# Attention and expert layer on one core: in the late attention steps VectorE computes three exponential tiles, ScalarE sixty in groups of three and one alone

## The reference, cut to what matters

```python
xn = layernorm(x)                                  # x: (4, 1024, 128)
q, k, v = heads(xn @ Wq.T), heads(xn @ Wk.T), heads(xn @ Wv.T)   # 16 heads of 8
q, k = rope(q), rope(k)
attn = softmax(einsum('bhnd,bhmd->bhnm', q, k) * 8 ** -0.5)
a = einsum('bhnm,bhmd->bhnd', attn, v)
gate = softmax(xn @ gate_w + gate_b); top 2 of 8 experts
f = sum over the two of gate * (three-layer expert with gelu)(xn)
return x + a + f
```

## Time and profile before

| | |
|---|---|
| median of 3 runs | 640.51 us (640.36 to 640.55) |
| profiled execution, its own time | 641.5 us |
| span of that execution (first to last instruction) | 639.8 us |
| instructions | 12291 |
| mean granted TensorE clock | 0.999 |

### The profile page before, as it was taken

The page is one execution under the profiler, slowest core; times in us unless marked ns, Lnnn a source line. Parts: engine busy times, 40 slices in busy tenths (PEclk is TensorE's granted clock), DMA queues, the critical chain, the costliest instruction groups (busy, mean ns, idle before and its releaser), DMA issues.

```text
span 639.8 us, 12291 instructions
## 1 busy us (share of the span) xinstructions
PE 599.6 (94%) x4152; PEld 260.1 (41%) x4152; DVE 239.1 (37%) x742; ACT 546.8 (85%) x555; POOL 166.9 (26%) x187
## 2 busy tenths in 40 slices
PE   9889999999999998998999999999898998999895
PEld 6323332222222222222999999982222222222221
DVE  5655224766352335022565556630202020211204
ACT  3799999999999998999555555569999999999994
POOL 2700000001444444531122221223332333323310
PEclk9999999999999999999999999999999999999999
DMA  7654611532464246783333333311212111121204
GB/s 226 182 181 163 233 34 50 198 138 99 149 210 149 91 140 227 246 260 82 81 76 74 74 74 74 74 37 42 71 44 69 58 58 57 62 77 42 71 13 135
DMA packets 82625, 70.74 MB, mean 111 GB/s; under 512 B 44288, under 2 KB 58400, under 8 KB 82576
## 3 DMA queue, kind: packets, MB, share of 16 engines
q1 hardware_dynamic: 76000, 56.34, 29.1%
q0 software_dynamic: 5856, 13.05, 6.6%
q10 hardware_dynamic: 720, 0.71, 0.5%
HBM read 32.92 MB, written 32.96 MB: 103 GB/s over the span
## 4 chain that ended last, share of the span: by engine, by line
PE 62%; ACT 17%; issue 12%; DMA 3%; DVE 3%; SPq 1%; POOL 1%; DVEq 1%; ACTq 0%; POOLq 0%
PE ps L1411 18%; ACT probs L663 15%; PE ps L1394 11%; PE ps L1343 10%; PE ps L1335 5%; PE ps L1356 5%; PE ps L1318 3%; PE ps L1262 2%; ACT probs L641 2%; DMA k_st<-k_d 2%; DMA work<-slots_y_d,slot_i 2%; PE ps L1298 2%; PE ps L1225 1%; PE ps L1196 1%; DVE x_all L1133 1%
## 5 line engine op out<-in xcount | busy, mean ns | idle before, releaser
L663 ACT ACTIVATE probs<-ps 128x1536 f32<-128x1536 f32 (+1 forms) x308 | 408.6, 1432 | 8.2 <-PE ps L1394 6.6
L1411 PE MATMUL ps<-probs,v_st 128*32 128x512 f32 x1792 | 238.7, 604 | 4.4 <-DVE v_st L789 3.2
L1394 PE MATMUL ps<-q_st,k_st 32*128 32x512 f32 x896 | 154.5, 494 | 22.4 <-ACT probs L663 18.3
L1394 PEld LDWEIGHTS ps<-q_st,k_st 32*128 32x128 f32 x896 | 57.9, 181 | 235.0 <-ACT probs L663 172.7
L677 ACT ACTIVATE work<-ps,work 128x256 f32<-128x256 f32 (+1 forms) x156 | 64.9, 455 | 60.4 <-PE ps L1343 60.2
L541 POOL DMA_INDIRECT slots_x_d<-xn_all,slot_i x64 | 62.9, 983 | 196.9 <-DVE expert_i L987 127.2
L579 POOL DMA_INDIRECT work<-slots_y_d,slot_i x64 | 60.6, 947 | 122.0 <-PE ps L1411 79.2
L1343 PE MATMUL ps<-work 128*128 128x256 f32 (+1 forms) x312 | 68.0, 361 | 0.0
L641 ACT ACTIVATE probs<-ps 128x1024 f32<-128x1024 f32 x64 | 60.6, 1034 | 3.7 <-PE ps L1298 2.7
L1411 PEld LDWEIGHTS ps<-probs,v_st 128*32 128x32 f32 x1792 | 35.6, 107 | 60.7 <-issue 54.5
L789 DVE COPY v_st<-v_all 128x128 f32<-128x128 f32 (+1 forms) x32 | 8.5, 265 | 131.3 <-PE ps L1411 131.3
(11 more groups left out here) (177 smaller groups left out, 379.0 us busy)
## 6 DMA issues: line engine op xcount, KB each, us to landing
k_d<-parts SPq DMA_DIRECT2D x8, 1024.0 KB, 5.7
q_d<-parts SPq DMA_DIRECT2D x8, 1024.0 KB
q_st<-q_d SPq DMA_DIRECT2D x30, 256.0 KB
k_st<-k_d SPq DMA_DIRECT2D x30, 256.0 KB
slots_x_d<-parts SPq DMA_DIRECT2D x5, 1024.0 KB, 7.4
work<-slots_x_d SPq DMA_DIRECT2D x128, 32.0 KB, 1.9
slots_y_d<-work POOLq DMA_DIRECT2D x32, 128.0 KB, 2.2
work<-work SPq DMA_DIRECT2D x24, 128.0 KB
```

Source lines behind the costliest of these rows:

```text
L663: nc.scalar.activation(group_probs(phase, g)[:, 0:size, :], group_slot(g)[:, 0:size * HALF].rearrange("p (h n) -> p h n", n=HALF), ACT.Exp ...
L1394: ins = nc.tensor.matmul(group_slot(g)[:, n * HALF:(n + 1) * HALF], k_st[32 * h:32 * h + ROWS, mt * P:(mt + 1) * P], q_st[32 * h:32 * h + ...
L1411: ins = nc.tensor.matmul(o_ps[32 * h:32 * h + 32, :], v_window(mt, h, half), group_probs(phase, half * HALF_GROUPS + g)[:, n, :], start=be ...
```

## The change

A late step has 22 groups before and 20 after. The four tiles of half 1, key block 0 are taken out of the groups; the other 60 tiles (`LATE_ITEMS`) run on across the halves in groups of three. TensorE makes the scores of the four tiles in turns 2 to 5, one each, into bank 7, each after the one before has been read. VectorE reads the first three (heads 0, 3, 2) with a scale, and computes their exponential over 1536 columns: it adds a large constant to get the whole part, subtracts to get the fraction, shifts the whole part into the exponent, runs a polynomial of degree 5 by Horner's rule (all normalised to a leading coefficient of one), and multiplies. ScalarE takes the fourth tile (head 1) from bank 7 by itself behind group 7. The constant factor that this leaves is matched by a bias of the same size in all of ScalarE's late exponentials (`exp_bias`, a column of one number); it drops out in the division. TensorE adds the four tiles' products in turn 17. Transposes move from turn 5 to turn 9; `normalise(t - 1)` now stands in VectorE's loop of step t, behind the chain. The loop is written out instead of being a loop of the program. Of the sums for the output, the three of a whole batch move into steps 11, 13 and 14, between `combine` and `copy_o`. In the last step the chain is split around the first `copy_o`.

```diff
+LATE_ITEMS = [(0, mt, h) for mt in range(MT) for h in range(HG)] + [(1, mt, h) for mt in range(1, MT) for h in range(HG)]
+LATE_GROUPS = len(LATE_ITEMS) // 3
+LATE_BLOCKS = [(0, mt) for mt in range(MT)] + [(1, mt) for mt in range(1, MT)]
+HELP_AT = 2
+HELP_HEADS = (0, 3, 2, 1)
+HELP_VALUES = 17
...
+        help_probs = probs[:, PROB_RING - 1]
...
             for t in range(SPLIT, STEPS - 1):
-                sp.wait_ge(S["scores_done"], group_units(t) + HALF_GROUPS)
+                sp.wait_ge(S["scores_done"], group_units(t) + (LATE_ITEMS.index((0, MT - 1, HG - 1)) // 3 + 1))
                 load_half(q_st, q_d, t + 1, 0, S["q0_loaded"])
...
-                sp.wait_ge(S["scores_done"], group_units(t) + GROUPS)
+                sp.wait_ge(S["scores_done"], group_units(t + 1))
                 load_half(k_st, k_d, t + 1, 1, S["kb_loaded"])
                 load_half(q_st, q_d, t + 1, 1, S["q1_loaded"])
...
+            def late_exps(t, first=False):
+                for g in range(LATE_GROUPS):
+                    act.wait_ge(S["scores_done"], group_units(t) + (g + 1))
...
+                    nc.scalar.activation(late_probs(g), group_slot(g).rearrange("p (h n) -> p h n", n=HALF),
+                                         ACT.Exp, bias=exp_bias[:], scale=SCALE).then_inc(S["exp_done"], 1)
+                    if g == HELP_AT + 5:
+                        act.wait_ge(S["help_scored"], (t - SPLIT) * HG + HG)
+                        nc.scalar.activation(help_probs[:, 0, :], aux_ps, ACT.Exp, bias=exp_bias[:], scale=SCALE).then_inc(S["help_exp"], 1)
...
-            with dve.Fori(SPLIT, STEPS - 1) as t:
+            def read_help(t):
+
+                for k in range(3):
+                    dve.wait_ge(S["help_scored"], (t - SPLIT) * HG + k + 1)
+                    nc.vector.tensor_scalar(he_s[:, k * HALF:(k + 1) * HALF], aux_ps, SCALE / math.log(2), None, ALU.mult)\
+                        .then_inc(S["help_read"], 1)
+
+            def help_exps(t, lo=0, hi=8):
+
+                for k in range(lo, hi):
+                    if k == 0:
+                        dve.wait_ge(S["help_read"], (t - SPLIT) * 3 + 3)
+                        ins = nc.vector.tensor_scalar(he_t, he_s, EXP_MAGIC, None, ALU.add)
+                    elif k == 1:
+                        ins = nc.vector.scalar_tensor_tensor(he_g, he_t, EXP_MAGIC, he_s, ALU.subtract, ALU.subtract)
+                    elif k == 2:
+                        ins = nc.vector.tensor_scalar(he_s.bitcast(I32), he_t.bitcast(I32), 23, None, ALU.logical_shift_left)
+                    elif k < 7:
+                        ins = nc.vector.scalar_tensor_tensor(he_p, he_g if k == 3 else he_p, EXP_COEFFS[k - 3], he_g, ALU.add, ALU.mult)
+                    else:
+                        nc.vector.scalar_tensor_tensor(help_probs[:, 1:HG, :].rearrange("p h n -> p (h n)"), he_p, EXP_COEFFS[4], he_s,
+                                                       ALU.add, ALU.mult).then_inc(S["help_made"], 1)
+                        return
+                    ins.then_inc(S["help_chain"], 1)
+                    dve.wait_ge(S["help_chain"], (t - SPLIT) * 7 + k + 1)
+
+            finished = {11: 0, 13: 1, 14: 2}
+            dve.wait_ge(S["x_scattered"], 16 * 2 * TILES)
+            for t in range(SPLIT, STEPS - 1):
+                read_help(t)
...
+                help_exps(t)
+                if t > SPLIT:
+                    normalise(t - 1)
+                combine(t - SPLIT)
+                if t in finished:
+                    finish_rows(finished[t] * BT, BT).then_inc(S["out_ready"], 1)
                 load_v(t + 1, 0)
-                combine(t - SPLIT)
                 copy_o(t)
                 load_v(t + 1, 1)
-                normalise(t)
 
             last = STEPS - 1
+            read_help(last)
+            help_exps(last, 0, 4)
+            normalise(last - 1)
             copy_o(last, 0)
+            help_exps(last, 4)
             normalise(last, (0,))
             combine(last - SPLIT, TILES - GATHER * (last - SPLIT))
-            dve.wait_ge(S["x_scattered"], 16 * 2 * TILES)
-            for b in range(B - 1):
-                finish_rows(b * BT, BT).then_inc(S["out_ready"], 1)
             finish_rows((B - 1) * BT, BT // 2).then_inc(S["out_ready"], 1)
...
+            def help_scores(t, k):
+
+                if k == 0:
+                    pe.wait_ge(S["q1_loaded"], t * 16 + 16)
+                    free_aux(aux_of_turn(t - 1))
+                else:
+                    pe.wait_ge(S["help_read"], (t - SPLIT) * 3 + k)
+                h = HELP_HEADS[k]
+                nc.tensor.matmul(aux_ps, k_st[32 * h:32 * h + ROWS, 0:P], q_st[32 * h:32 * h + ROWS, HALF:N],
+                                 start=True, stop=True).then_inc(S["help_scored"], 1)
...
+            def late_step(t, first=False, last=False):
+                for g in range(LATE_GROUPS):
+                    if g < LATE_GROUPS - 1:
+                        late_scores(t, g + 1, first=(first and g == 0))
                     elif not last:
+                        late_scores(t + 1, 0)
...
+                    if HELP_AT <= g < HELP_AT + HG:
+                        help_scores(t, g - HELP_AT)
+                    if g == HELP_AT + 7 and not first:
+                        turn(t - 1, 0, True)
+                    if g == 13 and last:
+                        turn(t, 0)
+                    if g == HELP_VALUES:
+                        help_values(t)
                     if g > 0:
+                        n = late_ending(g - 1)
+                        if n is not None:
+                            late_values(t, n, last)
+                    elif not first:
+                        late_values(t - 1, len(LATE_BLOCKS) - 1)
```

More of the change, by code:

```diff
@@ L11 @@
+import math
 import concourse.bass as bass
@@ L267, in build @@
         gath = part(0, 2 * GATHER * C).rearrange("p (k c) -> p k c", c=C)
+        he_s, he_t, he_g, he_p = (part(2 * GATHER * C + 3 * HALF * k, 3 * HALF) for k in range(4))
         ps = ctx.enter_context(nc.psum_tensor("ps", [P, 4096], F32))
@@ L1405, in group_values @@
                     pe.wait_ge(S["v_loaded"], t * 2 + (j // 4 + 1))
-                begins, ends = (mt == 0, mt == MT - 1) if apart else (j == 0, j == BLOCKS - 1)
+                if j == 0:
+                    pe.wait_ge(S["o_copied"], t)
+                for h in range(HG):
+                    g, n = divmod(HG * mt + h, 3)
+                    ins = nc.tensor.matmul(o_ps[32 * h:32 * h + 32, :], v_window(mt, h, half),
+                                           group_probs(phase, half * HALF_GROUPS + g)[:, n, :], start=(j == 0), stop=(j == BLOCKS - 1))
@@ new lines, in group_values, with step @@
+                ins.then_inc(S["pv_done"], 1)
+            def step(t, phase, last=False, joined=False):
+                for g in range(GROUPS):
+                    if g < GROUPS - 1:
+                        group_scores(t, g + 1)
+                    elif not last:
+                        group_scores(t + 1, 0)
+                    if g in JOB_PLACE:
+                        extra_piece(t, JOB_PLACE[g])
+                    if g > 0:
+                        j = block_ending_in(g - 1)
+                        if j is not None:
+                            group_values(t, j, phase)
+                    elif not joined:
+                        group_values(t - 1, BLOCKS - 1, 1 - phase)
@@ new lines, in late_scores @@
+            def late_scores(t, g, first=False):
+                items = LATE_ITEMS[3 * g:3 * g + 3]
+                if g == 0:
+                    pe.wait_ge(S["ka_loaded"], t * 16 + 16)
+                    pe.wait_ge(S["q0_loaded"], t * 16 + 16)
+                if (0, MT // 2, 0) in items:
+                    pe.wait_ge(S["kb_loaded"], t * 16 + 16)
+                if g >= 2 or not first:
+                    pe.wait_ge(S["exp_done"], group_units(t) + (g - 1))
+                for n, (half, mt, h) in enumerate(items):
+                    ins = nc.tensor.matmul(group_slot(g)[:, n * HALF:(n + 1) * HALF],
+                                           k_st[32 * h:32 * h + ROWS, mt * P:(mt + 1) * P],
+                                           q_st[32 * h:32 * h + ROWS, half * HALF:(half + 1) * HALF], start=True, stop=True)
+                ins.then_inc(S["scores_done"], 1)
@@ L1407, in group_values, with late_values @@
+            def late_values(t, n, apart=False):
+                half, mt = LATE_BLOCKS[n]
+                pe.wait_ge(S["exp_done"], group_units(t) + ((HG * n + HG - 1) // 3 + 1))
+                if n in (0, 4):
+                    pe.wait_ge(S["v_loaded"], t * 2 + (n // 4 + 1))
+                begins, ends = (n in (0, MT), n in (MT - 1, len(LATE_BLOCKS) - 1)) if apart else (n == 0, n == len(LATE_BLOCKS) - 1)
                 if begins:
@@ L1482, in _ @@
             pe.wait_ge(S["y_made"], SLOT_TILES + 1)
-            group_scores(SPLIT, 0, first=True)
+            late_scores(SPLIT, 0, first=True)
```

(12 more changed lines are left out.)

81 lines of the change are left out of this document (47 added, 34 removed).

## The result

The changed kernel takes **664.93 us** (median of 4 runs, 664.22 to 665.7) against 640.53 before (640.36 to 640.74): ratio 1.0381, 95% interval 1.0363 to 1.0399. The forecast was 638.8, with 643.5 as its upper end. The profiled execution has a span of 662.5 us.

The account below looks back on a forecast made before the run. ScalarE's queue of exponentials bounds the seven late attention steps: 189.7 + 6.8 + 3.4 + 0.9 + 0.15 = 200.95 us against 202.65, 1.7 less. Taken off the median of 640.51, that gives 638.8, range 633.5 to 643.5.

Parts of the forecast that it names:

- The bias tile costs nothing: ScalarE's late exponentials: taking their bias from a column adds no time, judged by a gelu of 0.475 us against 0.50.
- The wait grows to 1.2 us: Step boundary: TensorE's first value block waits for VectorE's copy of the attention bank, 1.2 us instead of some 0.4.
- v: The time when block 11's values end on TensorE, from which the prediction counts the boundary; values may start at v + 8.07.
- SyncE loads covered: Late loads of queries, now needed at group 2 instead of 11, still land in time, covered by 1.6 us.
- the sum: Late exponentials' predicted stretch: 189.7 + 6.8 + 3.4 + 0.9 + 0.15 = 200.95 us, with 1.13 lost per boundary.
- What a boundary wait costs: Boundaries between late steps: ScalarE loses 1.13 us at each of six, 6.8 in all.
- The output sums: Three whole-batch additions between combine and copy in steps 11, 13 and 14: 3 x 1.14 = 3.4 us.
- ScalarE's own pace without bias: Late exponentials started without loss: 1.331 us a full group, 27.10 a step, 189.7 over seven steps.
- rival 3: VectorE's chain is late for group 17's values; each further us costs 7, so 647 and more; chance 0.04.
- rival 2: Helper scores lengthen TensorE's path in groups 3 to 5; at 0.43 us each the time is 646.5; chance 0.19.
- Rival 1: The boundary gives nothing back: losses stay 3.6 us, gain 9.3, time 631.2 (half the loss about 635); chance 0.24.
- The forecast's own case: Late steps: ScalarE's saving mostly lost at boundaries and output sums, 1.7 us less, 638.8 (own range 637 to 641); chance 0.46.

Follow-up runs that it names:

- e1: The kernel before, with only the bias column added to its late exponentials: 653.84 us.
- e5: The changed kernel, with combine moved into the next step, between VectorE's reads of helper scores and its chain: 642.97 us.
- e6: e5 without the bias column, the factor taken out by a power of two in the polynomial's constants: 630.12 us.
- e12: The changed kernel without the bias column, a power of two in the constants making up for it, chain still eight operations: 656.39 us.
- e14: e12 with SyncE's two late loads held until the step's gathers have landed: 646.69 us.
- e9: e7 with two dummy products per step on TensorE ahead of the first helper score: 651.71 us.
- e7: The changed kernel with the three output sums put back behind the last step: 663.23 us.
- e13: The changed kernel, bias kept, with SyncE's two late loads held until the step's gathers have landed: 653.95 us.
- e3: The changed kernel with combine moved behind the next step's chain, so ten gathers come in a row: 682.17 us.
- e10: e3 with the late loops of ScalarE and TensorE written out: 641.87 us, one run.

## Why the prediction was wrong

1. **"The bias tile costs nothing"** is the step that failed most: 0.092 us for each of 147 exponentials, 13.5 us (the pace in e1; 12.85 us in e5 against e6). It rested on a line drawn through the mean records of the exponentials to 256 columns, beside which the gelu row looked cheap. The records of a full queue overlap and stretch, so they don't lie on one line with others. Records that start after an idle time show the price: 1.54 us with the bias (464.84), 1.45 without (e12, at 493.39). The Trainium skill, "ScalarE: Activation LUTs", section "What ACT_TABLE_LOAD costs", states some 93 ns for a `[128,1]` pointer operand; by that figure the estimate would have been 147 x 0.093 = 13.7 us more, a slower kernel. The runs agree with it.
2. **"The wait grows to 1.2 us."** It measured 1.13 and 1.30 at the first two boundaries, and was right by luck there; at the three boundaries with a sum it was 2.54 to 2.96. Without the bias it is 2.10 (e12): combine starts 5.3 us after v instead of 4.13. The prediction counted that TensorE asks one short slot earlier, but not that SyncE's loads, which wait for the step's last scores, come 1.4 us earlier against the gathers (0.35 us behind the last one instead of 1.78). "SyncE loads covered" looked at who waits for the loads, not at what they pass beside. With the loads moved (e14) combine starts after 4.11, and the steps at whole clock lose 1.07 to 1.55 us, where the sum had 1.13. In the changed kernel the slower ScalarE lets TensorE ask 0.7 us later (v + 7.79, where e12 has v + 7.06 and the sum had v + 6.88), and that hid it.
3. **What a boundary wait costs.** The prediction had 6.8 us for six, at whole clock. At whole clock they cost 7.6 (e9, 6 x 1.26). It had no term for the clock, which fell at every one of them (e7 to e9: 11.5 us). So even e14, without bias and without the collision, is at 646.69, above the range: its stretch is 207.2, 6.3 more than the sum, and three falls of the clock lie in it.
4. **The output sums**, 3.4 predicted, cost 4.8 us in the stretch (e7). That they cost nothing at the end was right before, and would not be here: 3 us of tail.
5. **What was right.** ScalarE's own pace without bias, 189.7 (1.331 a full group in e12; the estimate of 1.42 that the prediction worked out from the Trainium skill, "VectorE: DVE Perf Modes", did not hold); the two-input operations, 1.76 (1.75); tensor_scalar 0.96 (at most 1.12); the chain done 4.9 us before it is wanted, so rival 3 falls; the fourth score beside three starts 0.01 us later and scores with a helper score come 1.43 us apart in e6, so rival 2 falls as a cause; the last step loses 0.87 in e5 (0.9); tail 7.7 (8.2). Rival 1 named the right place with the wrong sign. The forecast's own case had the right boundary; its sum was wrong in the price of the bias, in a collision of transfers, and in the clock.

Still open: why the clock fell at some boundaries of e9, e12 and e13 and not at others (in e12 it stayed whole at a wait of 2.10 us), and how the 12.4 us of loss beyond the sum split between the clock, the collision and the longer wait at the sums, since each changes the others.

## What to carry to other kernels

Price every operand that an instruction gains from records that start after an idle time, not from the means of a full queue: 0.09 us on each of 147 instructions is 13.5 us, more than the 9.3 that ScalarE was to gain. When work moves, list also the transfers that keep their trigger, and see what they now pass beside. Where a new wait of a microsecond falls on TensorE at each step, price also a half-clock stretch behind it (here about 1.3 us each), and look first for an order in which the copy that frees its bank stands ahead of everything that waits for DMA (e5, e6).

## What the runs showed of the hardware beyond that

- *Gathers beside VectorE.* GpSimd's record of one gather is 0.95 us (e1: 947 ns mean); beside the chain it reaches 2.25 us in the changed kernel, while none of the 64 in the kernel before is over 1.02. The Trainium skill, "GPSIMD Engine Reference", section "Specifications", says that its SBUF interfaces are shared with VectorE, with contention when that reads two inputs. The trace agrees: every late gather of over 1.1 us overlaps a two-input operation of VectorE for a part of its time. The second gather below also overlaps a tensor_scalar for its 0.96 us, so the rows don't say what that one adds. Timeline of the changed kernel:

```profile
467.82 1.28 POOL L614 DMA_INDIRECT work<-slots_y_d,slot_i  x1 [4.32 <-PE ps L1558]
...
468.32 1.76 DVE L1213 SCALAR_TENSOR_TENSOR work<-work 128x1536 f32<-128x1536 f32 x1
...
469.41 1.79 POOL L614 DMA_INDIRECT work<-slots_y_d,slot_i  x1 [0.30 <-issue]
```

- *Loops beside a row of gathers*: ten gathers in a row cost 40 us with ScalarE's and TensorE's steps in loops (e3, 682.17) and nothing with them written out (e10, 641.87).
- *The clock without a long wait*: in e13 it fell at 444.8 us with waits of 0.5 and 0.9 us ahead of it, and at 465.3 us with waits of 0.84 and 0.36.
